# Two attention and mixture-of-experts blocks on one core: fp32r maxima, queries prepared inside the attention loop, one merged norm, other places for weight parts, table load and warm-ups

## The reference, cut to what matters

```python
x = x + _L0_xattn_ref(_layernorm(x), ctx, ...)   # x: (2, 512, 128), ctx: (2, 77, 128), 16 heads of 8
x = x + _L0_ffn_ref(_layernorm(x), ...)          # 8 experts, top 2, hidden 512
x = x + _L1_xattn_ref(_layernorm(x), ctx, ctx, ...)
x = x + _L1_ffn_ref(_layernorm(x), ...)          # 8 experts, top 2, capacity 321
# inside _L0_xattn_ref, on its input h and on ctx:
q_in = _layernorm(h) * gamma + beta              # a second norm of what is already normed
q = rope(q_in @ Wq.T); k = rope(kv_in @ Wk.T); v = kv_in @ Wv.T
scores = q @ k.T * SCALE + temporal_bias         # 512 x 77 a head; block 1 has no rope and no bias
attended = softmax(scores) @ v @ Wout.T + b_out
output = sigmoid(attended @ Wgate.T + b_gate) * attended + (1 - gate) * h    # block 1: plain projection
```

## Time and profile before

| | us |
|---|---|
| median of 3 runs | 326.11 |
| lowest, highest | 325.69, 334.38 |
| span of the profiled execution, first to last instruction | 324.3 |

### The profile page before, as it was taken

The page is one execution under the profiler, slowest core; times in us unless marked ns, Lnnn a source line. Parts: engine busy times, 40 slices in busy tenths (PEclk is TensorE's granted clock), DMA queues, the critical chain, the costliest instruction groups (busy, mean ns, idle before and its releaser), DMA issues.

```text
span 324.3 us, 5466 instructions
## 1 busy us (share of the span) xinstructions
PE 250.7 (77%) x2044; PEld 197.2 (61%) x2044; DVE 155.1 (48%) x497; ACT 118.2 (36%) x206; POOL 137.8 (42%) x178
## 2 busy tenths in 40 slices
PE   2767999999975539999942989989987338999800
PEld 2645766667754427999941775545555328999800
DVE  3878425363775364242211964276878303332205
ACT  4033637755321023443500067965540204423200
POOL 5744602630156441355562400641267631456640
PEclk9999999999975558999995799999999959999975
DMA  7999970200011017000013920200010125001015
GB/s 241 269 224 377 219 161 2 65 3 2 0 36 34 33 33 197 16 20 26 23 36 127 361 116 0 66 1 2 0 37 33 33 82 141 15 31 36 26 29 181
DMA packets 26819, 27.02 MB, mean 83 GB/s; under 512 B 3193, under 2 KB 23844, under 8 KB 26534
## 3 DMA queue, kind: packets, MB, share of 16 engines
q1 hardware_dynamic: 23797, 21.58, 24.6%
q0 software_dynamic: 2560, 4.08, 3.9%
q10 hardware_dynamic: 432, 0.98, 0.9%
HBM read 16.76 MB, written 10.79 MB: 85 GB/s over the span
## 4 chain that ended last, share of the span: by engine, by line
PE 49%; issue 20%; DVE 13%; DMA 6%; POOL 5%; ACT 3%; another core or an unknown queue 1%; SPq 1%; POOLq 0%; DVEq 0%; ACTq 0%
PE ps L1201 8%; PE ps L1406 6%; PE ps L1178 6%; PE ps L1395 5%; PE ps L1162 4%; PE ps L1153 4%; PE ps L1133 3%; PE ps L1184 2%; DMA xres<-x 2%; DMA xe<-back 2%; DVE cst L813 2%; DMA sent<-hidk,slotu 1%; DVE attT L814 1%; PE ps L1217 1%
## 5 line engine op out<-in xcount | busy, mean ns | idle before, releaser
L559 POOL DMA_INDIRECT back<-probT,pairu x48 | 46.5, 970 | 37.4 <-DVE probT L992 15.1
L1133 PE MATMUL ps<-blank,ident 128*128 128x256 f32 x90 | 28.6, 479 | 23.6 <-DMA sent<-hidk,slotu 13.0
L1406 PE MATMUL ps<-w,hT 128*128 128x128 f32 (+1 forms) x384 | 45.0, 274 | 0.0
L804 DVE TENSOR_REDUCE peak<-ps 128x8 f32<-128x616 f32 x32 | 25.5, 798 | 40.2 <-PE ps L1153 40.2
L1406 PEld LDWEIGHTS ps<-w,hT 128*128 128x128 f32 (+1 forms) x384 | 44.2, 183 | 0.0
L654 ACT ACTIVATE probT<-ps 77x1024 f32<-77x1024 f32 x32 | 32.7, 1022 | 27.7 <-PE ps L1184 15.5
L518 POOL DMA_INDIRECT sent<-hidk,slotu x32 | 31.9, 997 | 16.4 <-issue 9.8
L1133 PEld LDWEIGHTS ps<-blank,ident 128*128 128x128 f32 x90 | 21.1, 244 | 28.5 <-issue 14.0
L531 POOL TENSOR_TENSOR w1lo<-hT,w1hi 128x1024 fp32r<-128x1024 f32 x8 | 18.9, 2366 | 40.0 <-ACT w1hi L628 40.0
L1178 PE MATMUL ps<-qst,kst 100*78 100x256 f32 x128 | 29.1, 300 | 1.0 <-ACT qst L638 1.0
L500 POOL TENSOR_SCALAR vare<-mv 128x2 f32<-128x2 f32 (+2 forms) x17 | 3.8, 226 | 52.8 <-DVE mv L786 52.3
(11 more groups left out here) (158 smaller groups left out, 474.1 us busy)
## 6 DMA issues: line engine op xcount, KB each, us to landing
sent<-blank SPq DMA_DIRECT2D x16, 193.5 KB, 8.5
xe<-sent SPq DMA_DIRECT2D x16, 193.5 KB, 4.0
back<-blank SPq DMA_DIRECT2D x16, 128.0 KB, 4.8
hT<-w1b SPq DMA_DIRECT2D x4, 512.0 KB, 6.0
w<-w2b SPq DMA_DIRECT2D x1, 2048.0 KB, 13.5
xe<-back SPq DMA_DIRECT2D x8, 256.0 KB, 3.5
hT<-w1d SPq DMA_DIRECT2D x4, 512.0 KB, 5.5
w<-w2d SPq DMA_DIRECT2D x1, 2048.0 KB, 11.4
```

The lines of the kernel that those rows point to most:

```text
L559: pool.indirect_dma_start(back[m], bass.IndirectOffsetOnAxis(ap=pairu[0:n, e, c:c + 1], axis=0), ye[0:n, e, c, :], None, bounds_check=NPAI ...
L804: dve.tensor_reduce(peak[:, u % 2], s, AX.X, ALU.max, negate=True).then_inc(s_peak[a], 1)
L1133: pe.matmul(ps[:, bank, 0:GQ], ident[:], blank[:, 0:2, 0:D], start=True, stop=True)
L1406: last = pe.matmul(ps[0:n, 6 + e % 2, c * P:(c + 1) * P], hT[:, e % 2, f, c * P:c * P + n], w2[:, e, f, :], start=(f == 0), stop=(f == FC ...
```

## The change

- `peak` and the identity become fp32r (`identr`), so the maxima are fp32r matmuls; they go to a bank of their own (`BMX`), and attended numerators and denominators share one bank (`BND`), which lets the queries' work have bank `BY` in the loop.
- Only group 0 (block 0: and the tokens of group 1) is prepared ahead of the loop; the query steps of groups 1 to 3 stand in turns 0 to 9. The rope sum and low part move from GpSimd to VectorE, the bias factors' split from VectorE to GpSimd.
- Block 0's second norm is taken from the first statistics: its deviation is (v(1 + e) + e*e)^-0.5, with `rtwice` for the merged norm, `rstd` for the first norm, which is now done in turns 1 and 4 (`own_norm`).
- Weight parts in turns 5, 6, 7, 9 and 3, 4, 5, 7. Due steps of groups 0 to 2 come a turn later in most places, and where several are due, those of group 3 go last.
- The exp table is loaded ahead of the query steps. Warm-ups: 6 for 13 at the start; 3 when the rows are back and 5 when the first group is gathered for 12; and 1 to 3 ahead of some steps of the first group.

```diff
-WARM_START = 13
-WARM_SUM = 12
+WARM_START = 6
+WARM_BACK = 3
+WARM_SUM = 5
+WARM_QUERIES = [dict(tokens=1, queries=0, keys=0, stack=3, scores=2), dict(tokens=0, queries=1, stack=2, scores=1)]
...
+PE_STEPS = [dict(project3=4, gate3=5, project=5, gate=8, turn=10, logits=11, ranks=12, next_context=8, next_parts=10,
+                 next_keys=11, turn3=8, logits3=9, ranks3=10),
+            dict(project3=4, project=5, turn3=7, logits3=7, ranks3=9, turn=8, logits=8, ranks=10)]
+DVE_STEPS = [dict(attended=5, projected3=6, residual3=7, hidden3=9, projected=9, residual=10, hidden=11,
+                  choose=13, slots=14, next_context=11, next_parts=13, next_keys=14, choose3=11, slots3=12),
+             dict(attended=5, residual3=7, hidden3=8, choose3=10, slots3=11, residual=8, hidden=9, choose=11, slots=12)]
...
+PE_QUERIES = [[(-1, "tokens", 0), (-1, "queries", 0), (-1, "tokens", 1), (-1, "keys", 0), (-1, "stack", 0),
+               (0, "queries", 1), (1, "tokens", 2), (3, "stack", 1), (4, "queries", 2), (4, "tokens", 3),
+               (6, "stack", 2), (7, "queries", 3), (9, "stack", 3)],
+              [(-1, "tokens", 0), (-1, "queries", 0), (-1, "stack", 0), (0, "tokens", 1), (1, "queries", 1),
+               (3, "stack", 1), (4, "tokens", 2), (5, "queries", 2), (6, "stack", 2), (7, "tokens", 3),
+               (8, "queries", 3), (9, "stack", 3)]]
...
+DVE_QUERIES = [[(-1, "rotated", 0), (-1, "values", 0), (-1, "low", 0), (-1, "keys", 0), (-1, "stack", 0),
+                (0, "norm", 1), (0, "rotated", 1), (1, "hidden", 0), (2, "low", 1), (3, "stack", 1),
+                (4, "rotated", 2), (4, "hidden", 1), (5, "low", 2), (5, "keys", 1), (6, "stack", 2),
+                (7, "rotated", 3), (8, "low", 3), (9, "stack", 3)],
+               [(-1, "sum", 0), (-1, "sum", 1), (-1, "norm", 0), (-1, "norm", 1), (-1, "low", 0), (-1, "stack", 0),
+                (0, "sum", 2), (1, "norm", 2), (2, "low", 1), (3, "stack", 1), (3, "sum", 3), (4, "norm", 3),
+                (5, "low", 2), (6, "stack", 2), (8, "low", 3), (9, "stack", 3)]]
+
+WEIGHT_TURNS = [[5, 6, 7, 9], [3, 4, 5, 7]]
...
-        peak = sb("peak", [P, 2, GT, Q4])
+        peak = sb("peak", [P, 2, GT, Q4], F32R)
...
+            def twice_normed(b):
+
+                s = of_batch(b)
+                count[0] += 1
+                pool.wait_ge(s_var, count[0])
+                link(pool.tensor_scalar(vtwice[:, s], mv[:, s, 1], 1.0 + EPS, EPS * EPS, ALU.mult, ALU.add))
+                pool.tensor_tensor(rtwice[:, s], vtwice[:, s], power[:, s], ALU.pow).then_inc(s_rstd, 1)
...
             for a in range(2):
+                if a == 0:
+                    act.wait_ge(s_iset, 8)
+                load_table(ACT.Exp, 2 + a)
                 query_steps(a, -1)
-                load_table(ACT.Exp, 2 + a)
...
                 for i in range(GT):
-                    last = pe.matmul(ps[ST:ST + Q4, BK + u % 2, i * P:(i + 1) * P], peak[:, u % 2, i, :], ident[:],
-                                     start=True, stop=True)
+                    at = GQ * (u % 2) + i * P
+                    last = pe.matmul(ps[0:Q4, BMX, at:at + P], peak[:, u % 2, i, :], identr[:], start=True, stop=True)
...
             def stack_q(a, g):
 
                 pe.wait_ge(s_qlo, GROUPS * a + g + 1)
-                if a == 0 and g == 1:
-                    pe.wait_ge(s_kvfree, 1)
+                if g >= 1:
+                    pe.wait_ge(s_qstD, GROUPS * a + g)
+                    pe.wait_ge(s_inT, min(g + 2, GROUPS) if a == 0 else GROUPS + g + 1)
...
+            pe.wait_ge(s_back[0], 16 * E * SC)
+            warm_up(WARM_BACK, BMX)
             pe.wait_ge(s_got[0], 16)
-            warm_up(WARM_SUM)
+            warm_up(WARM_SUM, BMX)
```

More of the change, by code:

```diff
@@ L64 @@
 W_NAMES = ["q0", "q0p", "k0", "k0p", "v0", "out0", "gate0", "q1", "k1", "v1", "o1"]
[L71 to L101, removed]
@@ new lines @@
+ACT_QUERIES = [[(-1, "tokens", 0), (-1, "tokens", 1), (-1, "high", 0), (-1, "keys", 0), (-1, "stack", 0),
+                (1, "tokens", 2), (1, "high", 1), (2, "stack", 1), (4, "high", 2), (4, "tokens", 3),
+                (5, "stack", 2), (7, "high", 3), (8, "stack", 3)],
+               [(-1, "tokens", 0), (-1, "high", 0), (-1, "stack", 0), (0, "tokens", 1), (1, "high", 1),
+                (2, "stack", 1), (3, "tokens", 2), (4, "high", 2), (5, "stack", 2), (6, "tokens", 3),
+                (7, "high", 3), (8, "stack", 3)]]
@@ L114, in due @@
         g, rest = divmod(u - delay - (UG - 1), UG)
[L115 to L118, removed]
+        if name[-1] != "3" and rest == 0 and 0 <= g < GROUPS and not (g == GROUPS - 1 and name + "3" in steps):
             yield name, g
+    for name, delay in steps.items():
+        if name[-1] == "3" and u == UNITS - 1 + delay:
+            yield name[:-1], GROUPS - 1
 def bias_factors():
@@ L589, in _ @@
             for b in range(B):
-                deviations(of_batch(b))
-            for g in range(GROUPS):
-                rotary_sum(g)
-                low_queries(g)
+                twice_normed(b)
+            for b in range(B):
+                once_normed(b)
+            bias_parts()
             pool.wait_ge(s_rows, 64)
@@ L939, in next_parts @@
                 if g == GROUPS - 1:
-                    keys_and_values(1)
+                    keys(1)
+                    values(1)
             def next_keys(m, g):
@@ L1144, in scores @@
                 b, at, j = place(u)
+                if a == 0 and u == 0:
+                    pe.wait_ge(s_inT, 2)
                 if j == 0:
@@ L1335, in query_steps @@
                 for name, g in at_turn(PE_QUERIES[a], turn):
+                    if turn < 0 and g == 0:
+                        warm_up(WARM_QUERIES[a][name], BS)
                     if name == "tokens":
@@ L1346, in attention @@
                 query_steps(a, -1)
+                warm_up(WARM_QUERIES[a]["scores"], BS)
                 scores(a, 0)
```

215 lines of the change are left out of this document (116 added, 99 removed).

## The result

The changed kernel took 336.42 us (median of 4 runs, 330.97 to 342.36) against 326.20 us before: 1.022 times as long, 95% interval 1.014 to 1.030. Beside other kernels on one chip later it was 1.013 (1.004 to 1.021). So it is slower, though whether by 2% the interval leaves open. Medians here are of all executions of a kernel, the ratios compare its fast runs alone, those within 1.5% of its fastest. The forecast was 315.6, range 307 to 322. The profiled run of after is its fastest: 330.97 us, a span of 329.2 us at a mean granted clock of 0.842; before had 324.3 us at 0.898. The longer runs of after have the lower clocks, if not in strict order: 0.842, 0.814, 0.819 and 0.797 for 331.0, 335.2, 337.6 and 342.4 us.

The account below looks back on a forecast made before the run. Loops were taken as bound by TensorE's work, starts and tails by chains through all engines. -8.4 (to block 0's loop end) + 2.8 - 6.2 + 0.3 + 1.0 = -10.5, giving 315.6 us; own range 312 to 319, whole range 307 to 322.

Parts of the forecast that it names:

- the price of the waits: In both loops, waits added to TensorE's sum of work: 1.6 us in block 0, 3.5 us in block 1.
- rival (c): TensorE's clock stays low through both starts and each loop's first 6 us: +15, 331 us; chance 0.05.
- Maxima: In both loops, fp32r maxima take two passes for four, saving 0.39 us a unit: 5.85 us a block.
- Rival (d): The fp32r maxima save nothing, since narrow weights, not streaming, are the price: 326 us; chance 0.04.
- Block 0's start: Ahead of block 0's loop: the first shifted scores start at 24.0 instead of 32.21 us, -8.2.
- Block 0's loop: TensorE's sum from first shifted scores to last attended values falls 1.8 us, plus 1.6 us of waits.
- Block 0's tail: Behind block 0's loop: later projections and group 3's projection behind group 2's gate cost +2.8 us (0 to +4.5).
- Block 1's start: Ahead of block 1's loop: fewer warm-ups, earlier table load and fewer steps before the first peak, -6.2 us.
- Its loop: Block 1's loop: TensorE's work -3.25 us, lost time in units and weight parts +3.5 (0 to +5), sum +0.3.
- Its tail: Block 1's tail: last projection behind group 2's turn and logits +1.7, a norm no longer ahead -0.7, +1.0 us.
- (a): TensorE's sums alone decide: the waits in both loops vanish and the tail loses 1, 307.5 us; chance 0.20.
- (b): VectorE's queue sets the loops: half of 16 us of added work exposed, plus contention and upper-end tails, 321.6 us; chance 0.18.

Follow-up runs that it names:

- s1: The changed kernel unaltered, run again beside others on one chip: 334.90 us, 1.013 of the kernel before.
- e4: The kernel before with VectorE reading unused columns twice ahead of its maxima in unit 5 of each block: 358.08 us, ratio 1.096.
- e5: The kernel before with the same two VectorE reads in unit 5, plus seven throw-away TensorE matmuls ahead of its wait for those maxima: 338.13 us.
- e1: The kernel before with the single-pass fp32r maxima alone, in a bank of their own: 313.96 us, ratio 0.961; again on one chip 315.54 us, 0.965.
- e11: The changed kernel with all queries ahead of both loops and the warm-ups, tails and weight turns of before: 320.86 us, ratio 0.955.
- e2: The changed kernel with GpSimd's low weight parts at turns 8 to 11 in both blocks, behind the query steps: 331.92 us, 1.010 of before.
- e9: Changed kernel, block 0 weight parts late, its groups 1 to 3 at before's tail delays, block 1 queries ahead of loop: 316.7 us, 0.945; again 313.28 us, 0.949.
- e8: The changed kernel with block 0's weight parts at turns 8 to 11 and block 1's queries ahead of the loop, tail and weight turns as before: 317.62 us.
- e3: The changed kernel with five throw-away matmuls ahead of each stacking in the loops: 330.86 us, 1.012 of before.
- e6: The kernel before with VectorE reading unused columns once ahead of its maxima in unit 5 of each block: 330.18 us.

## Why the prediction failed

**The step that failed** is the price of the waits. I wrote "To it come waits", took 1.6 us for block 0 and 3.5 us for block 1, each wait at its own length, and gave the half clock to rival (c) alone, at 0.05, as a matter of the starts ("the clock is low at the first stacking of both blocks"). There the clock was full. It fell inside the loops, behind waits of the kind that I had counted: 14 us at 1.2 GHz in each block's loop of the profiled run, 31 us in block 1's of s1. The loops came out 12.1 us longer than forecast, and the length of the waits is the small part of that: in the two loops they add up to 4.3 and 5.4 us, against 0.6 and 2.9 in before, 6.1 more where I had charged 4.1 (1.6 and 3.5, less the 1.0 that goes). The other 10 us go with 28 us at half clock in the two loops, which by an estimate cost up to half their length. Rival (c) has the right engine and the right kind of cost, but in the wrong place, and its total, 331 us, is near the profiled run's by luck. The trace of before could have made me ask: its loops hold the clock at 1.0 with 94 to 99% of TensorE's time busy, its half-idle tail has 0.55, so the rows showed both states. They didn't show where between them the change would land. e4 against e5 shows what the clock can cost: 32.6 us in the two loops against 6.1 with the same waits filled.

**Maxima:** right. Forecast -5.85 us a block; e1's loops give -5.7 and -6.8, and with the starts counted in -4.7 and -6.2. Rival (d) is out.

**Block 0's start:** -9.6 measured for -8.2, by the chain that I walked through, faster by 1.4 us up to the stacking (tokens at 12.99, right behind the router's landing, for 13.6; the stacking at 17.7 for 19.05). I had credited the merged norms with part of it; e11 shows that they give nothing without the moved queries.

**Block 0's loop:** forecast -0.2 in length, measured +6.5. Without the contention (e2, clock full) it is -1.5, so the sum of TensorE's work and small waits was sound, even 1.3 us too careful. I had put the contention at 0.5 us, "0 to 2", and reasoned from the length that a blocked instruction loses, "1.3 each, in slack mostly". It lost 2.0 each, twice in a row, on the way to a stacking for which TensorE waits. The rule that I quoted from the Trainium skill (GPSIMD Engine Reference, Specifications: VectorE instructions with two SBUF inputs or in a two-port mode) held for both rows above, and e2's blocked norm, with one SBUF input, could fall only under its second half, which I had left out of my count; that it runs in such a mode no run shows.

**Block 0's tail:** +4.2 for +2.8, inside its bounds; e9 gives 4 us of it back, as it should if the order is the reason, but its loop is 3.5 us longer than e8's.

**Block 1's start:** -5.2 for -6.2. **Its loop:** +5.7 for +0.3, the clock again, as the rows of half clock show; with these steps out of the loop e8 takes 41.5 us. No run took the waits alone away here, as e2 did in block 0; the nearest is e3, whose fillers ahead of the stackings shortened the low stretch from 14 to 3 us. **Its tail:** +3.4 for +1.0. There TensorE runs at 1.2 GHz from 243 to 249 and 256 to 262 us, and four warm-ups stand ahead of group 2's turn and four ahead of group 3's ranks, 3.76 us each time at that clock.

**The rivals (a) and (b):** (a) didn't come; even e1's loops, which keep the full clock, hold 2.2 and 2.9 us of waits. Its sum was also wrong: both tails stand in it with +1.0 where I had priced them at +3.8, and less the 1 us that it names it gives 309.3, not 307.5. (b) named the right engine, VectorE, in front of the right waits, and stopped at their length, 321.6 us.

What stays open: how long a low stretch lasts. It ended after 14 us in after and 31 us in s1 with equal waits ahead. Open too is which wait brings it. e8 and e9 have the same waits at 22 to 27 us (0.4, 0.6, 0.3 and 0.6 us), at which the clock fell in e9 and not in e8; a wait of 1.9 us ahead of block 0's first shifted scores is followed by 3 us of half clock in e4 and e6 and by none in before; one of 1.2 us in block 0's loop is followed by 3 us in e11 and by none in e1. Only inside the loops did it fall at every wait of 1.8 us or more (e4, after, s1, e2). So the mean loss can be measured, but the loss of one run can't be read off the order of its instructions. Also open is whether e5's fillers could be fewer.

## What to carry to other kernels

Where a loop keeps TensorE busy without a gap, its clock is part of the bound: count a new wait not only at its length but also at what a stretch of half clock behind it would cost (here 13 to 20 us for waits of 1.8 and 2.3 us, nothing for others of up to 1.6 in e1). A short start that moves its steps into the loop can lose more there than it gains: in block 1 it lost 12 us for 6. It isn't always so; in block 0, once the weight parts were out of the way, start and loop together took 81.8 us against e1's 86.1 on the same chip. Before steps of another engine go into such a loop, look at what runs on GpSimd beside them, and move the two apart by turns. And when a change has several parts, try the one whose gain is surest alone: here it had most of the gain (0.965 against 0.949 for the best kernel).

## What was not expected of the hardware

- With a single wait of TensorE of 1.8 us came 24 us at 1.2 GHz, with TensorE 93% busy or more all the while (e4: 7.46 and twice 8.00 of 8 us); with one of 2.3 us, 44 us. Waits of 0.2 and 0.8 us in e6 and of 1.6 us in e1 did nothing.
- TensorE, busy nearly without a gap, stayed at 1.2 GHz for 14 us in one run and for 31 us in another of the same program.
- Some VectorE instructions that start beside GpSimd's 2.4 us subtraction end just behind it: 2.42 and 2.36 us for 0.42 (two SBUF inputs), and 4.67 us for 0.6 across two subtractions back to back (two instructions with one SBUF input and per-partition scalars). Peaks (PSUM input, 0.80 us) and reciprocals (one SBUF input, 1.74 us) kept their time beside it.
- Before took 326.3, 330.1, 337.6 and 327.6 us (medians; the lowest runs 323.9, 325.1, 329.1 and 324.1) on four chips: differences of one or two per cent between kernels need the same chip.
